# A decoder layer on one core: the start of attention loaded and issued in halves, two tag batches moved to VectorE, the experts' first gathers moved into the routing block

## The reference

```python
x = _layernorm(x + _L0_attn_ref(x, L0_attn_w_in, L0_attn_w_out))          # causal, ALiBi slopes
x = _layernorm(x + _L0_xattn_ref(x, ctx_1024, ctx_1024, Wq, bq, ..., Wo, bo))
x = _layernorm(x + _L0_ffn_ref(x, Wr, br, W1, b1, W2, b2))

# _L0_ffn_ref: 8 experts, the best 2 of each token, room for cap = ceil(1.2 * N / 8) tokens each
probs = jax.nn.softmax(x @ Wr + br, axis=-1)
gates, ids = jax.lax.top_k(probs, K)
order = jnp.lexsort((-flat_g, flat_ids))     # by expert, then by falling gate
xg = x[disp_tok].reshape(E, cap, Dm)         # rows gathered for each expert
h = jax.nn.silu(jnp.einsum('ecd,edh->ech', xg, W1) + b1[:, None, :])
out = jnp.einsum('ech,ehd->ecd', h, W2) + b2[:, None, :]
y = jnp.zeros((N, Dm)).at[disp_tok].add(gated)
```

## Time and profile before

| | |
|---|---|
| three runs | 1656.23 us median (1655.02 to 1657.7) |
| the profiled execution | 1653.82 us, span 1652.1 us |
| TensorE matmul / weight load busy | 1416.3 us (86%) / 1194.4 us (72%) |
| VectorE / ScalarE / GpSimd busy | 1025.9 (62%) / 1011.4 (61%) / 599.5 (36%) |
| mean granted TensorE clock | 0.928 |

### The profile page before, as it was taken

The page is one execution under the profiler, slowest core; times in us unless marked ns, Lnnn a source line. Parts: engine busy times, 40 slices in busy tenths (PEclk is TensorE's granted clock), DMA queues, the critical chain, the costliest instruction groups (busy, mean ns, idle before and its releaser), DMA issues. The chain is left out here.

```text
span 1652.1 us, 43736 instructions
## 1 busy us (share of the span) xinstructions
PE 1416.3 (86%) x17866; PEld 1194.4 (72%) x17866; DVE 1025.9 (62%) x2311; ACT 1011.4 (61%) x1555; POOL 599.5 (36%) x607
## 2 busy tenths in 40 slices
PE   5999999999999999999998561128999999999940
PEld 3777777777777777777776441118999999999940
DVE  4666666666677777777777368874454545545425
ACT  3677777777777777777776350176565555556407
POOL 1554544444443232323231000014455445545236
PEclk8999999999999999999999785558999999999975
DMA  5021212121212222222221461003443443343239
GB/s 186 21 60 60 60 60 60 55 64 51 61 53 70 70 83 73 80 77 79 79 66 51 134 173 12 0 11 104 97 104 52 95 96 74 69 97 50 25 74 355
DMA packets 127862, 129.52 MB, mean 78 GB/s; under 512 B 26352, under 2 KB 114528, under 8 KB 127664
## 3 DMA queue, kind: packets, MB, share of 16 engines
q1 hardware_dynamic: 112560, 106.24, 21.0%
q0 software_dynamic: 15104, 20.48, 7.8%
HBM read 82.53 MB, written 44.16 MB: 77 GB/s over the span
## 5 line engine op out<-in xcount | busy, mean ns | idle before, releaser
L501 ACT ACTIVATE at_pr<-at_A 128x2048 f32<-128x2048 f32 x128 | 240.8, 1881 | 148.6 <-PE at_A L328 148.6
L595 DVE TENSOR_REDUCE at_mx<-at_A 128x12 f32<-128x1536 f32 x128 | 224.6, 1755 | 67.9 <-PE at_A L293 64.2
L35 PE MATMUL ex_D<-ex_w,ex_hT 128*128 128x256 f32 (+1 forms) x1920 | 234.3, 282 | 0.3
L35 PEld LDWEIGHTS ex_D<-ex_w,ex_hT 128*128 128x128 f32 (+1 forms) x1920 | 231.0, 184 | 2.9 <-DVE ex_raw L1459 1.7
L35 PE MATMUL ex_U<-ex_xT,ex_w 128*128 128x384 f32 (+1 forms) x1152 | 224.2, 354 | 0.0
L1513 POOL DMA_INDIRECT total<-ex_o,ids x80 | 131.8, 1647 | 229.0 <-DVE ex_o L1464 197.3
L35 PEld LDWEIGHTS ex_U<-ex_xT,ex_w 128*128 128x128 f32 x1152 | 208.3, 190 | 8.4
L732 POOL TENSOR_SCALAR_AFFINE_SELECT at_pr<-at_pr 128x2048 f32<-128x2048 f32 x64 | 128.6, 2009 | 210.4 <-ACT at_pr L501 210.3
L1497 POOL DMA_INDIRECT ex_xg<-rows,ids x80 | 102.5, 1281 | 203.2 <-DVE ex_xg L1467 179.1
L1449 DVE TENSOR_TENSOR ex_hT<-ex_h,ex_hT 128x384 fp32r<-128x384 f32 (+1 forms) x192 | 112.7, 587 | 99.1 <-ACT ex_hT L1409 99.1
L631 DVE TENSOR_TENSOR at_oT<-at_C,at_oT 128x512 fp32r<-128x512 f32 x64 | 44.3, 692 | 165.7 <-ACT at_oT L514 165.7
(11 more groups left out here) (196 smaller groups left out, 2685.4 us busy)
## 6 DMA issues: line engine op xcount, KB each, us to landing
w_in<-in_w SPq DMA_DIRECT2D x16, 1024.0 KB, 6.3
at_turned<-in_x_turned SPq DMA_DIRECT2D x16, 512.0 KB, 4.6
at_x<-in_x SPq DMA_DIRECT2D x16, 512.0 KB, 4.0
x<-at_y SPq DMA_DIRECT2D x32, 256.0 KB, 2.4
at_x<-x SPq DMA_DIRECT2D x16, 512.0 KB, 3.9
at_turned<-in_ctx_turned SPq DMA_DIRECT2D x16, 512.0 KB, 4.8
rows<-at_y SPq DMA_DIRECT2D x32, 256.0 KB, 2.2
total<-at_y SPq DMA_DIRECT2D x32, 256.0 KB, 3.4
```

The source lines that it names most:

```text
L35: last = nc.tensor.matmul(out, pick_l(left, a), pick_r(right, b), start=(start and n == 0), stop=(stop and n == 2))
L501: nc.scalar.activation(pr[:, k % 2].rearrange("p i n a q -> p (i n a q)"), A[:].rearrange("p i n a q -> p (i n a q)"), ACT.Exp).then_inc(e ...
L595: nc.vector.tensor_reduce(mx[:, k % 2, 0:12], A[:, 0:3].rearrange("p i n a k -> p (i n a) k"), AX, ALU.max).then_inc(max_done, 1)
```

## The change

**Start of attention.** SyncE issues wq, x, wk, then the small tables, wv, one table, x of group 1, wo, the last table, and only then the plain x. VectorE clears a tile `warm` and splits wq and wk (`split_weights`), makes the tables for the maxima, splits wv and wo, and makes the last tables. TensorE multiplies the cleared tile 20 times into a bank that nobody reads. Then come q, k, q, the maxima of set 0, and the second k; the v products go into the loop, between the maxima of set 1 and the scores of set 0. ScalarE follows that order.

**Routing.** Batches 3 and 7 of the tags are made by VectorE in one instruction each. The clearing of `xg` moves to the head of VectorE's list in `route_block`. GpSimd gets a list in `route_block`: it waits for that, for the stored gates and for `ids`, and issues the gathers of the first three chunks. `xg` and its semaphores are made outside the two blocks.

**Experts.** Chunk 1 is turned after the first four pieces of chunk 0's first product, on TensorE, ScalarE and VectorE alike.

```diff
+            load_weight(0, "wq", qk_in)
             load_turned(0)
-            for i, name in enumerate(("wq", "wk", "wv", "wo")):
-                sp.dma_start(w_stage[:, i], w_self[name].rearrange("(t p) n -> p t n", p=P)).then_inc(w_in, 16)
+            load_weight(1, "wk", qk_in)
             sp.dma_start(q_scale[0][:], consts["q_scale_self"]).then_inc(small_in, 16)
             sp.dma_start(ident[:], consts["ident"]).then_inc(ident_in, 16)
-            sp.dma_start(stage[:, 2048:2560], consts["sel32_causal"]).then_inc(table_in, 16)
+            sp.dma_start(stage[:, 0:896], consts["past_tabs"]).then_inc(table_in, 16)
             sp.dma_start(stage[:, 2560:2688], consts["rows32_causal"]).then_inc(table_in, 16)
-            sp.dma_start(stage[:, 2688:3200], consts["sel32"]).then_inc(table_in, 16)
-            sp.dma_start(stage[:, 0:896], consts["past_tabs"]).then_inc(table_in, 16)
+            load_weight(2, "wv", vo_in)
+            sp.dma_start(stage[:, 2048:2560], consts["sel32_causal"]).then_inc(sel_in, 16)
+            load_turned(1)
+            load_weight(3, "wo", vo_in)
+            sp.dma_start(stage[:, 2688:3200], consts["sel32"]).then_inc(sel_in, 16)
             load_x(0)
-            load_turned(1)
...
-            pe.wait_ge(ident_in, 16)
+            pe.wait_ge(warm_made, 1)
+            for _ in range(WARM):
+                nc.tensor.matmul(C[1][:, :], warm[:, 0:P], warm[:, :], start=True, stop=True)
             pe.wait_ge(w_ready, 1)
             project_q(0, 0)
             project_k(0, 0)
             project_q(0, 1)
+            pe.wait_ge(tables_ready, 1)
+            maxima(0)
             project_k(0, 1)
-            project_v(0, 0)
-            project_v(0, 1)
-            pe.wait_ge(tables_ready, 1)
+            pe.wait_ge(ident_in, 16)
+            pe.wait_ge(tables_ready, 2)
             pe.wait_ge(v_ready, 1)
-            maxima(0)
...
+                if k == 0:
+                    pe.wait_ge(w_ready, 2)
+                    project_v(0, 0)
+                    project_v(0, 1)
+                    pe.wait_ge(tables_ready, 3)
...
+            def split_weights(first, last, signal, done):
+                dve.wait_ge(signal, 32)
+                for i in range(first, last):
+                    ins = nc.vector.tensor_copy((wq, wk, wv, wo)[i][0][:, 0], w_stage[:, i])
+                ins.then_inc(hi_done, 1)
+                dve.wait_ge(hi_done, done)
+                for i in range(first, last):
+                    ins = nc.vector.tensor_tensor((wq, wk, wv, wo)[i][0][:, 1], w_stage[:, i],
+                                                  (wq, wk, wv, wo)[i][0][:, 0].bitcast(FP32), ALU.subtract)
+                ins.then_inc(w_ready, 1)
...
             for b in range(Q // BATCH):
                 part, kth = divmod(b, 2)
+                if b % DVE_TAGS == DVE_TAGS - 1:
+                    continue
                 act.wait_ge(rows_hit, b + 1)
...
+                if b % DVE_TAGS == DVE_TAGS - 1:
+                    dve.wait_ge(rows_hit, b + 1)
+                    v.tensor_tensor(tagged[:, qs, :], hit_row[:, qs, :],
+                                    tag[:, part * BATCH:(part + 1) * BATCH].unsqueeze(2).to_broadcast([P, BATCH, ROWS]),
+                                    ALU.mult).then_inc(dve_tags, 1)
...
+            v.memset(xg[:, :, parts[-1] - 1, :], 0.0).then_inc(cleared, 1)
...
+        @block.gpsimd
+        def _(pool):
+            _, _, starts, _, tiles_of = chunks_of(cap)
+            pool.wait_ge(cleared, 1)
+            pool.wait_ge(gates_stored, 16)
+            pool.wait_ge(ids_made, 1)
+            for s in range(AHEAD):
+                for b, (_, n) in enumerate(tiles_of[s]):
+                    at = starts[s] + b
+                    nc.gpsimd.indirect_dma_start(xg[0:n, s, b, :], None, rows_dram,
+                                                 bass.IndirectOffsetOnAxis(ap=ids[0:n, 0, at:at + 1], axis=0),
+                                                 bounds_check=rows_dram.shape[0] - 1).then_inc(x_loaded[s], 16)
...
             def body(e, j, ch):
                 nx = shifted(e, j, ch, 1)
+                if first_steps(e, ch, 1):
+                    up(e, j, ch, 0, UP)
+                    transpose_x(*nx)
+                    up(e, j, ch, UP, HT)
+                    return
                 if exists(nx[0], 0):
                     transpose_x(*nx)
                 up(e, j, ch)
...
-            for s in range(AHEAD):
-                gather(s)
```

More of the change, by code:

```diff
@@ L83, in attention_layers @@
         minus_half = sb("minus_half", [P, 2])
+        warm = sb("warm", [P, G], BF16)
         q_scale = [sb(f"q_scale{i}", [P, 2]) for i in range(2)]
@@ L662, in _ @@
+            nc.vector.memset(warm[:], 0.0).then_inc(warm_made, 1)
             nc.vector.memset(v[:, :, :, :, DK + 1:VW], 0.0)
             nc.vector.memset(v[:, :, :, :, DK:DK + 1], 1.0).then_inc(v_ready, 1)
-            dve.wait_ge(w_in, 64)
-            for i, wt in enumerate((wq, wk, wv, wo)):
-                ins = nc.vector.tensor_copy(wt[0][:, 0], w_stage[:, i])
-            ins.then_inc(hi_done, 1)
-            dve.wait_ge(hi_done, 1)
-            for i, wt in enumerate((wq, wk, wv, wo)):
-                ins = nc.vector.tensor_tensor(wt[0][:, 1], w_stage[:, i], wt[0][:, 0].bitcast(FP32), ALU.subtract)
@@ L920, in _, with route_block @@
             take(groups - 1)
[L923 removed]
+def route_block(nc, tiles, cap, logits, rows_dram, ids, first_weights, first_rows, consts):
     LT = -(-cap // P)
@@ L1197, in experts_block @@
     tiles_of = [[(o, min(P, n - o)) for o in range(0, n, P)] for n in widths]
+    return NC, parts, starts, widths, tiles_of
+def experts_block(nc, cap, rows_dram, ids, first_weights, first_rows, sum_dram, w, consts):
+    LT = -(-cap // P)
+    NC, parts, starts, widths, tiles_of = chunks_of(cap)
     W = max(widths)
@@ L1231, in experts_block @@
         small_in = sem("small_in")
-        x_loaded = [sem(f"x_loaded{i}") for i in range(XG)]
-        cleared = sem("cleared")
         t_full = sem("t_full")
@@ L1334, in transpose_x, with up @@
                     last.then_inc(t_full, 1)
-            def up(e, j, ch):
+            def up(e, j, ch, first=0, last_m=HT):
                 s = e * NC + ch
@@ L1341, in up @@
                 pe.wait_ge(x_lo, (s + 1) * 2)
-                for m in range(HT):
+                for m in range(first, last_m):
                     wait(pe, u_done, s * HT + m - UP + 1)
@@ L1398, in body @@
                 nx = shifted(e, j, ch, 1)
-                if exists(nx[0], 0):
+                if exists(nx[0], 0) and s > 0:
                     round_x(*nx)
@@ L1403, in body @@
                 for m in range(HT):
+                    if s == 0 and m == UP:
+                        round_x(*nx)
                     act.wait_ge(u_full, s * HT + m + 1)
@@ L1442, in rest_w, with rest_h @@
                 nc.vector.tensor_tensor(dst[:, j, 1], src[:], dst[:, j, 0].bitcast(FP32), ALU.subtract).then_inc(w_lo, 1)
-            def rest_h(e, j, ch):
+            def rest_h(e, j, ch, first=0, last=HT):
                 s = e * NC + ch
                 n = widths[ch]
-                for m in range(HT):
+                for m in range(first, last):
                     dve.wait_ge(u_done, s * HT + m + 1)
@@ L1619, in moe @@
         w_in = c.enter_context(nc.semaphore("w_in"))
+        xg = c.enter_context(nc.sbuf_tensor("xg", [P, XG, NB, D + E], FP32))
+        x_loaded = [c.enter_context(nc.semaphore(f"x_loaded{i}")) for i in range(XG)]
         logits_block(nc, tiles, rows, total, ins["wr"], ins["br"], ins["ident"], logits)
-        route_block(nc, tiles, cap, logits, rows, ids, (w1_in, w2_in, w_in), ins)
-        experts_block(nc, cap, rows, ids, (w1_in, w2_in, w_in), total, {k: ins[k] for k in ("w1", "w2", "b1", "b2")}, ins)
+        route_block(nc, tiles, cap, logits, rows, ids, (w1_in, w2_in, w_in), (xg, x_loaded), ins)
+        experts_block(nc, cap, rows, ids, (w1_in, w2_in, w_in), (xg, x_loaded), total, {k: ins[k] for k in ("w1", "w2", "b1", "b2")}, ins)
     norm_block(nc, tiles, total, out)
```

63 lines of the change are left out of this document (40 added, 23 removed).

## The result

The change is faster: 1649.74 us, the median of six runs (1649.2 to 1650.23), against 1656.16 for the kernel before in the same series (six runs, 1655.02 to 1657.7), ratio 0.9962, 95% interval 0.995 to 0.9974. That is 6.4 us, about 0.4%, where I had forecast 0.85 us and given 0.48 to "within 0.2%". The profiled run of the change took 1650.23 us, its span is 1648.3, so the two profiles differ by only 3.8 us in the span. Where the other 2.6 us come from is the second question of the experiments.

The account below looks back on a forecast made before the run. TensorE was taken as the bound over most of the span, with gains possible only at the start and between routing and experts: -10.8 - 1.1 + 11.05 = -0.85, profiled 1653.0, median 1655.4 us, range 1653 to 1658.

Parts of the forecast that it names:

- Part 1: Start of attention: reordered loads, splits and warming products bring the third set's maxima earlier; -10.8 us.
- the warm case: Start of attention: TensorE's clock stays up over the pause after the warming products; gain 11.3 us, against 10.3 cold.
- Part 2: Routing: VectorE tagging two of eight batches gains 2.0 us, the moved clearing costs 0.9; together -1.1 us.
- Part 3: Routing to experts: all engines wait at the barrier for ten gathers; with the later turn of chunk 1, +11.05 us.
- The close: End of the routing block: from the last gather's instruction until the next block opens, taken as 4.3 us, bounds 0.5 and 6.6.
- The +0.85 of the later turn: Experts' first product: chunk 1's six transposes now stand inside it, after the clock has risen; +0.85 us.
- the row of 2.82: Experts: a profiled gather beside a weight subtraction took 2.82 us; used to put ten undisturbed gathers at 13.0, not 15.7.
- the last one: Whole kernel: the median stays 2.4 us above the profiled time, so 1653.0 profiled becomes 1655.4.
- cheap close: Rival, end of the routing block: GpSimd's close costs 0.5 us instead of 4.3; -4.65, 1651.6 us; chance 0.24.
- Dear close: Rival, end of the routing block: ten gathers take 15.7 us and the close 6.6; +4.15, 1660.4 us; chance 0.16.
- the clock falls: Rival, start of attention: the clock drops after the first maxima, costing some 4 us more; 1659.5 us; chance 0.06.
- the barrier holds nobody: Rival, routing to experts: no engine waits for GpSimd's gathers at the barrier; -18.55, 1637.7 us; chance 0.06.

Follow-up runs that it names:

- e14: The kernel before, unedited, timed and profiled again in a later series: 1655.82 us, ratio 1.0.
- e13: The change, unedited, timed and profiled again in the same series as e14: 1651.54 us, ratio 0.9972 to the kernel before.
- e12: e7 with the rest of the first x made by VectorE instead of GpSimd: 1639.06 us, ratio 0.9902 to the kernel before.
- e6: The kernel before, unedited, profiled a second time, in a series without the stall: 1653.00 us.
- e7: e4 with expert 1's weights loaded only after chunk 0's first product: 1638.12 us, ratio 0.9913 to the kernel before.
- e16: e7 run again, unedited, in the same series as e14: 1640.99 us, ratio 0.9916 to the kernel before.
- e3: The change with gathers and clearing back in the experts' block, chunk 1 still turned later: 1645.26 us, ratio 0.9941 to the kernel before.
- e2: The kernel before with only the start of attention changed: 1645.62 us, ratio 0.9941 to the kernel before.
- e4: e3 with the gathered tile cleared by GpSimd in the routing block: 1641.49 us, ratio 0.9918 to the kernel before.
- e17: The change with only chunk 0's three gathers in the routing block, the other seven in the experts' block: 1642.90 us, ratio 0.9936 to the kernel before.

## Why the prediction was wrong

The table sets the moments of two pairs of profiles beside each other: the first of each kernel, and e14 and e13 from one series. The differences are change less before.

| moment | first pair | diff | e14, e13 | diff |
|---|---|---|---|---|
| third set's maxima | 38.14, 26.00 | -12.1 | 38.15, 27.82 | -10.3 |
| first product of the logits | 939.59, 927.91 | -11.7 | 939.76, 929.25 | -10.5 |
| first comparison of the tags | 1067.38, 1057.66 | -9.7 | 1067.60, 1058.11 | -9.5 |
| ids | 1106.03, 1094.22 | -11.8 | 1106.25, 1094.67 | -11.6 |
| experts' first product | 1122.38, 1118.89 | -3.5 | 1122.61, 1119.25 | -3.4 |
| turn of chunk 2 | 1132.92, 1129.34 | -3.6 | 1133.12, 1130.83 | -2.3 |
| turn of chunk 3 | 1150.95, 1147.37 | -3.6 | 1153.27, 1148.86 | -4.4 |
| norm block | 1602.94, 1599.08 | -3.9 | 1605.18, 1600.63 | -4.5 |

**Part 1, right in its mechanism.** -10.8, between 11.3 warm and 10.3 cold; measured 12.1 with the clock held, 10.3 with it fallen. The pause came (2.21 to 3.73 us for 2 to 3); the clock fell in it in two of three profiles, at a price near the 1 us (from the first real product to maxima(0) 4.66 us warm, 5.94 in e13). TensorE's first real product came at 10.07 and 10.62 for the 10.65, which is some 0.6 of the 0.8 by which the warm case was too low. What shifts it between profiles is when x and wk land, and whether the clock lasts. In the first pair 1.0 us of it was then given back in the logits, where TensorE had to wait longer for its full clock (the turns of 16 blocks took 3.65 us instead of 3.36, the first logits 1.86 instead of 1.08; the granted clock was still 0.50 from 932 to 934, when these ran; in the kernel before it was 0.87 from 942 to 944). The prediction had nothing for that, and in the first pair the two errors cancel by luck.

**Part 2, right.** From the first comparison to the ids 36.56 us instead of 38.65: 2.09 gained for the 2.0. The clearing cost its 0.9.

**Part 3, one term mis-sized.** Start of the gathers 1.04 (0.93 forecast), ten gathers 13.19 (13.0), close 2.37 (4.3), then 7.81 (8.1): 24.4 us for the 26.3. The close was taken from the end of the experts, by "only the part after landing can't be the transfer". Here the block opens 2.2 to 2.4 us after the last gather's instruction, about 1 after the landing. What makes it 4.3 after the scatters wasn't tried. The +0.85 of the later turn came as +1.1 in the second pair and not at all in the first, where the clock rose sooner (granted 1.00 from 1122 to 1124; 0.50 in e13). A gather beside VectorE's subtraction did take 3.03 us, so the row of 2.82 was the right one to believe. By the Trainium skill (same page and section) the subtraction would leave the descriptors alone; the trace does not agree, with 3.03 beside and 1.01 without.

**The step that failed most is the last one.** "The median of the three runs is 2.4 higher, 1656.2, so the profiled time becomes 1653.0 and the median 1655.4". That carried the distance between one profile and the median over to the changed kernel as if it were noise. It was a stage, as far as the runs show: the profile was of an execution without the stall, while before has it where its median is like that of the timed runs (2.1 us in e14), and the change does not. The timed runs themselves left no trace, so that they had it is inferred. Sum of the two for the second pair: -0.85, less 1.9 for the close, is -2.75, where it shows -2.3 at chunk 2's turn; less 2.1 for the stall -4.85, where it ends 4.5 apart, and the medians of three series 4.3 to 6.4. In the first pair neither profile has the stall: -2.75, less the 0.85 of the later turn that didn't come there, is -3.6, and it shows -3.6 at chunk 2's turn and -3.8 in the span. So even the profiled time, 1650.2 for the 1653.0, was missed, and by the close above all.

The rival "cheap close" had the time nearest to the result by the profile (a close of 0.5, -4.65), but by luck: the close was 2.4, halfway between its 0.5 and my 4.3. "Dear close", "the clock falls" (at 1659.5) and "the barrier holds nobody" are refuted by the rows above. The largest statement stands: two large terms of opposite sign, and the gathers ahead of the barrier were a loss. Without part 3 the same change is 11.6 us faster than before instead of 4.3 to 6.4, and with the later turn, the clearing by GpSimd, the late load and the rest on VectorE together (e12) 16.5.

## What to carry to other kernels

Work moved ahead of a barrier is paid by all engines: before a transfer is issued early, ask who else stands at the end of that block, and whether the block waits for the transfer to land (here each gather cost all engines 1.32 us and the close 2.3 more). Where a profile's time lies outside the range of the timed runs, don't carry the difference over to the new kernel: take the profile again and find the stage it lies in. An edit that fills an idle engine can hold up another one (a subtraction of 0.68 us took 2.71): look for the same instruction with two durations.

## What the hardware showed that I had not expected

The same program spends 1 to 4 us more in one place in some series (2.1 in the kernel before, e6 against e14; 3.5 in e7's, against e16): ScalarE waits up to 2.4 us with TensorE's products on time (in e3 0.41 and 0.97 us ahead of the casts of the turned chunk, 2.37 and 0.41 ahead of silu), early in the experts only, never in the 20 later chunks, whose turns repeat to 0.1 us in all profiles. Why is open. And the order of issue decides who is held up: the cast of wk, with one input, took 2.56 us in e13, where GpSimd's subtraction had begun 0.19 us before it, and 0.42 in the change's first profile, where it began 0.06 us ahead of GpSimd, which then held up the subtraction behind it. In e2, e4 and e17 it was the cast of wq that began behind GpSimd's subtraction of 2.34 us, by 0.23, 0.58 and 1.44 us, and it took 2.39, 2.04 and 1.19, until just after that ended.
